# A graph and attention program on one Trainium2 core: a load that is waited for later, a third tile of probabilities, and PSUM banks cleared by two-column products

## What is computed

```python
def _gcn(x, W, b, row, col, ew):            # twice, in the third layer
    x = x @ W
    deg = segment_sum(ew, col) + 1.0
    dinv = rsqrt(deg)
    norm = dinv[row] * ew * dinv[col]
    return segment_sum(norm[:, None] * x[row], col) + (dinv * dinv)[:, None] * x + b
h = relu(x @ Wd + bd) @ Wu + bu + x          # the adapter, ahead of the convolutions
...
attn = softmax(einsum('bhsd,bhtd->bhst', Q, Kt) / sqrt(64))     # fourth layer, 12 heads
attn_out = einsum('bhst,bhtd->bhsd', attn, V)
```

## Time and profile before

| | us |
|---|---|
| timed runs: median (lowest to highest) of 3 | 3585.93 (3583.48 to 3592.32) |
| profiled execution, its own time | 3583.17 |
| its span, first to last instruction | 3581.5 |
| busy in it: TensorE / its weight loads | 2892.7 / 2540.3 |
| busy in it: VectorE / ScalarE / GpSimd | 2028.6 / 1270.8 / 265.5 |
| mean granted TensorE clock (1 is 2.4 GHz, 0.5 is 1.2 GHz) | 0.899 |

### The profile page before, as it was taken

The page is one execution under the profiler, slowest core; times in us unless marked ns, Lnnn a source line. Parts: engine busy times, 40 slices in busy tenths (PEclk is TensorE's granted clock), DMA queues, the critical chain, the costliest instruction groups (busy, mean ns, idle before and its releaser), DMA issues. The chain is left out here.

```text
span 3581.5 us, 42656 instructions
## 1 busy us (share of the span) xinstructions
PE 2892.7 (81%) x15884; PEld 2540.3 (71%) x15885; DVE 2028.6 (57%) x2844; ACT 1270.8 (35%) x1928; POOL 265.5 (7%) x232
## 2 busy tenths in 40 slices
PE   6664887877877859969999986968798699799777
PEld 5553677876877858938888973746666576788776
DVE  6654477877877832253333342363299355688754
ACT  1222275565665521121112110022199101566520
POOL 1332030030030000000000001000000000111100
PEclk9988898988988979979999996978899698899988
DMA  0012111111111172101010022013454120443223
GB/s 29 14 29 50 47 36 59 36 47 59 36 47 59 38 175 52 39 4 51 26 53 26 26 69 53 0 44 120 140 128 88 45 87 0 94 101 76 46 61 91
DMA packets 83081, 204.39 MB, mean 57 GB/s; under 512 B 9866, under 2 KB 39164, under 8 KB 81700
## 3 DMA queue, kind: packets, MB, share of 16 engines
q1 hardware_dynamic: 82950, 202.56, 21.2%
HBM read 153.80 MB, written 44.89 MB: 55 GB/s over the span
## 5 line engine op out<-in xcount | busy, mean ns | idle before, releaser
L831 PE MATMUL ps<-h,e_gat_aggregate 125*125 125x193 f32 x2400 | 408.3, 333 | 90.0 <-DVE e_gat_aggregate L815 73.9
L831 PEld LDWEIGHTS ps<-h,e_gat_aggregate 125*125 125x125 f32 x2400 | 401.8, 192 | 96.8 <-DVE e_gat_aggregate L815 77.8
L103 PE MATMUL ps<-w_pair_experts,hidden_experts 128*125 128x384 f32 x1440 | 257.6, 338 | 5.3 <-DVE x L1237 3.5
L103 PE MATMUL ps<-ln_turned,w_pair_experts 128*128 128x512 f32 (+1 forms) x1296 | 252.0, 356 | 9.4 <-DVE w_pair_experts L1221 9.4
L103 PEld LDWEIGHTS ps<-w_pair_experts,hidden_experts 128*125 128x125 f32 x1440 | 250.7, 185 | 10.5 <-DVE x L1237 6.2
L103 PEld LDWEIGHTS ps<-ln_turned,w_pair_experts 128*128 128x128 f32 x1296 | 212.0, 190 | 50.7 <-DVE w_pair_experts L1221 12.2
L103 PE MATMUL ps<-gat_w_pair_gat_scores,x_turned 128*125 128x384 f32 x1080 | 199.0, 348 | 39.1 <-DVE gat_w_pair_gat_scores L689 38.6
L103 PEld LDWEIGHTS ps<-gat_w_pair_gat_scores,x_turned 128*125 128x125 f32 x1080 | 197.2, 193 | 40.7 <-DVE gat_w_pair_gat_scores L689 39.3
L813 DVE TENSOR_TENSOR e_gat_aggregate<-e_gat_aggregate 125x1250 f32<-125x1250 f32 x120 | 175.2, 1460 | 87.4 <-DMA gat_bias_gat_aggregate<-in_gat_b 48.5
L314 PE MATMUL ps<-dst_hot_build_adjacency,src_hot_build_adjacency 125*125 125x128 bf16 x2380 | 186.1, 235 | 43.4 <-DVE dst_hot_build_adjacency L267 42.4
L777 ACT ACTIVATE e_gat_aggregate<-row_gat_aggregate,from_src 125x1250 f32<-125x1250 f32 x120 | 160.7, 1339 | 166.9 <-PE ps L831 139.3
(11 more groups left out here) (312 smaller groups left out, 4895.4 us busy)
## 6 DMA issues: line engine op xcount, KB each, us to landing
stock<-in_moe_w SPq DMA_DIRECT2D x16, 1152.0 KB, 6.3
row_gat_aggregate<-r_scratch SPq DMA_DIRECT2D x24, 625.0 KB, 6.5
V_home<-q_scratch SPq DMA_DIRECT2D x48, 312.5 KB, 6.5
rows_dense_rows_from<-node_scratch SPq DMA_DIRECT2D x10, 1080.0 KB
stock<-in_gat_w SPq DMA_DIRECT2D x4, 2304.0 KB, 8.5
q_scratch<-V_home SPq DMA_DIRECT2D x6, 1250.0 KB, 4.5
k_scratch<-V_home SPq DMA_DIRECT2D x6, 1250.0 KB, 4.5
V_home<-k_scratch SPq DMA_DIRECT2D x24, 312.5 KB, 6.3
```

The source lines that it names most:

```text
L103: last = pe.matmul(out, left(x), right(y), start=start and n == 0, stop=stop and n == 2)
L831: last = pe.matmul(ps[0:TP, bank(head, d // 2), d % 2 * (C + 1):(d % 2 + 1) * (C + 1)], e[:, n % 3, 0, d * TP:(d + 1) * TP], h[:, t, head, :],
```

## The change

Three edits that don't touch one another:

1. The tile of zeros is 125 x 125 instead of 125 x 512, and each clearing product writes two columns of its bank instead of 512. It still carries `start=True`.
2. The adjacency is no longer in `later`; SP issues its two transfers behind those, with a semaphore of their own (`adj_in`), and doesn't wait for them. VectorE waits for it at the head of `graph_convolutions`.
3. `p`, `p_high`, `p_low` have three buffers (`AHEAD`), TensorE's order is scores(0) to scores(2), and then scores(n+3), weigh(n), the waits hold at n-3, and ScalarE evacuates a head behind the exp of its third following tile (n % 10 == 2) instead of the second.

```diff
-    zeros = ph.sb("zeros", [TP, BANK], BF16)
+    zeros = ph.sb("zeros", [TP, TP], BF16)
...
-                        pe.matmul(ps[0:TP, 3 * odd + b, :], zeros[:, 0:TP], zeros[:], start=True, stop=False,
+                        pe.matmul(ps[0:TP, 3 * odd + b, 0:2], zeros[:], zeros[:, 0:2], start=True, stop=False,
...
             for to, source in later:
                 sp.dma_start(to, source).then_inc(later_in, 16)
+            if behind is not None:
+                to, source, done = behind
+                move_rows(sp, to, source, done)
             if later:
                 sp.wait_ge(later_in, 16 * len(later))
...
         def _(v):
             step = Chain(v, v_step)
+            v.wait_ge(adj_in, 32)
             for t in range(NT):
...
-                (adj[0:EVEN], a_rows[0:EVEN]), (adj[EVEN:TP], a_rows[EVEN:TP])])
+                behind=(adj, a_scratch.rearrange("(t p) d -> p t d", p=TP), adj_in))
...
-    p = ph.sb("p", [TP, 2, NQ])
+    AHEAD = 3
+    p = ph.sb("p", [TP, AHEAD, NQ])
...
-            scores(0)
-            scores(1)
+            for n in range(AHEAD):
+                scores(n)
             for n in range(LAST + 1):
-                if n + 2 <= LAST:
-                    scores(n + 2)
+                if n + AHEAD <= LAST:
+                    scores(n + AHEAD)
                 weigh(n)
...
-                if n >= 2:
-                    a.wait_ge(split, n - 1)
+                if n >= AHEAD:
+                    a.wait_ge(split, n - AHEAD + 1)
...
-                if n % NT == 1 and n >= NT:
+                if n % NT == 2 and n >= NT:
                     evacuate(n // NT - 1)
...
-                if n >= 2:
-                    v.wait_ge(p_used, n - 1)
+                if n >= AHEAD:
+                    v.wait_ge(p_used, n - AHEAD + 1)
```

More of the change, by code:

```diff
@@ L340, in tile_stats, with layernorm_turned @@
     return last
-def layernorm_turned(nc, g, x, turned, gamma=None, beta=None, x_in=None, later=(), stats_there=False):
+def layernorm_turned(nc, g, x, turned, gamma=None, beta=None, x_in=None, later=(), stats_there=False, behind=None):
     ph = Phase(nc, g, "layernorm_turned")
@@ L1853, in attend @@
     ps = g["ps"]
-    p = ph.sb("p", [TP, 2, NQ])
-    p_high = ph.sb("p_high", [TP, 2, NQ], F32R)
-    p_low = ph.sb("p_low", [TP, 2, NQ], F32R)
+    AHEAD = 3
+    p = ph.sb("p", [TP, AHEAD, NQ])
+    p_high = ph.sb("p_high", [TP, AHEAD, NQ], F32R)
+    p_low = ph.sb("p_low", [TP, AHEAD, NQ], F32R)
     k_both = ph.sb("k_high_low", [128, 2, N], F32R)
@@ L1947, in weigh @@
                     for b in range(3):
-                        last = pe.matmul(ps[:, RING + b, 0:PIECE], V[:, t, head, :], tile[:, n % 2, b * PIECE:(b + 1) * PIECE],
+                        last = pe.matmul(ps[:, RING + b, 0:PIECE], V[:, t, head, :], tile[:, n % AHEAD, b * PIECE:(b + 1) * PIECE],
                                          start=(t == 0 and part == 0), stop=(t == NT - 1 and part == 1))
                 last.then_inc(p_used, 1)
-            scores(0)
-            scores(1)
+            for n in range(AHEAD):
+                scores(n)
             for n in range(LAST + 1):
-                if n + 2 <= LAST:
-                    scores(n + 2)
+                if n + AHEAD <= LAST:
+                    scores(n + AHEAD)
                 weigh(n)
@@ L1974, in _ @@
                     bank = (first + at) % RING
-                    last = a.activation(spread(p[:, n % 2, :])[:, at:end, :], ps[0:TP, bank:bank + end - at, 0:PIECE], ACT.Exp, scale=-1.0)
+                    last = a.activation(spread(p[:, n % AHEAD, :])[:, at:end, :], ps[0:TP, bank:bank + end - at, 0:PIECE], ACT.Exp, scale=-1.0)
                 last.then_inc(exp_done, 1)
-                if n % NT == 1 and n >= NT:
+                if n % NT == 2 and n >= NT:
                     evacuate(n // NT - 1)
@@ L1993, in _ @@
                 else:
-                    v.tensor_copy(p_high[:, n % 2, :], p[:, n % 2, :]).then_inc(high_v, 1)
+                    v.tensor_copy(p_high[:, n % AHEAD, :], p[:, n % AHEAD, :]).then_inc(high_v, 1)
                     v.wait_ge(high_v, n - n // 3 + (0 if n % 3 == 2 else 1))
-                v.tensor_tensor(p_low[:, n % 2, :], p[:, n % 2, :], p_high[:, n % 2, :].bitcast(F32), ALU.subtract).then_inc(split, 1)
+                v.tensor_tensor(p_low[:, n % AHEAD, :], p[:, n % AHEAD, :], p_high[:, n % AHEAD, :].bitcast(F32), ALU.subtract).then_inc(split, 1)
     ph.end()
@@ L2205, in build @@
             a_rows = a_scratch.rearrange("(t p) d -> p t d", p=TP)
+            adj_in = gcn.enter_context(nc.semaphore("adjacency_in"))
             layernorm_turned(nc, g, x, g["xT"], later=[
```

12 lines of the change are left out of this document (7 added, 5 removed).

## The result

The changed kernel takes 3557.04 us (median of 4 runs, 3554.03 to 3561.45) where the kernel before took 3585.94 beside it (4 runs, 3583.48 to 3592.32): a ratio of 0.9918, 95% interval 0.99 to 0.9935, so 23 to 36 us faster. The prediction said 3522, with a range of 3504 to 3544. The profiled execution took 3556.27 us.

What follows compares the result with a forecast made beforehand. Stages follow one another behind barriers, so each edit was priced by who waits for whom in its own stage: -13 - 26.4 - 24.5 = -64, giving 3519 us in the profile and 3522 as a median, range 3504 to 3544.

Steps and rivals of the forecast that it cites:

- Edit 2, -26.4: Layer norm ahead of the adapter: the stage ends with ScalarE's work, no longer with the adjacency load, saving 26.4 us.
- the cover of the adapter: Before the convolutions: the adapter's 42 us of matmuls hide the moved wait for the load, with 17.5 us to spare.
- Edit 3, -24.5, bounds -10 and -25: Attend: a third tile gives VectorE's split 2.28 us more lead over GpSimd's adds, saving 24.5 us, between 10 and 25.
- the 20: Attend: of TensorE's 21.6 us of waits for VectorE's split, 20 us go.
- Edit 1, -13: Adjacency: clearing two columns in place of 512 lets later pairs start sooner, saving 13 us.
- Fewer products, lower clock in the adjacency: Rival: less TensorE work drops its clock; at half throughout, +24 for edit 1, total -27, 3559 us; chance 0.10.
- The price of sooner clearing with the clock held: Adjacency: 3.6 us in 14 full-clock windows, 10 in 11 half-clock windows, 0.5 in the last; sum 14, taken as 13.
- GpSimd sets the pair behind the first at full clock: Adjacency: GpSimd's operations hold VectorE's, so sooner clearing saves 0 in about 15 full-clock windows, 0.26 us in 14.
- full clearing: Rival, adjacency: the clearing pays in full, -26 for edit 1, total -77, 3509 us; chance 0.10.
- attend without its lead: Rival, attend: VectorE never regains its lead, so edit 3 gives only -12, total -51, 3535 us; chance 0.13.
- small loads late: Rival, ahead of the adapter: small loads land with the adjacency, edit 2 gives nothing, total -38, 3548 us; chance 0.03.
- GpSimd's addition starved: Rival, attend: GpSimd's add gets in only when VectorE rests, making the kernel slower, +68, 3654 us; chance 0.02.

Runs made afterwards that it cites:

- e2: The kernel before with only the adjacency load taken out of the layer norm's wait: 3558.6 us, ratio 0.9928.
- e5: The changed kernel with three 512-column products of zeros, serving nothing, added behind each adjacency window: 3536.5 us, ratio 0.9864.
- e7: The changed kernel with six 512-column products of zeros, serving nothing, added behind each adjacency window: 3520.3 us, ratio 0.9815.
- e10: The changed kernel with 512-column clearing as before, plus three 512-column products of zeros behind each adjacency window: 3529.6 us, ratio 0.9845.
- e12: The changed kernel with nine 512-column products of zeros, serving nothing, added behind each adjacency window: 3530.2 us, ratio 0.9847.
- e8: The kernel before without GpSimd's two sums per adjacency window, ScalarE copying one of three weight parts instead (result incomplete): 3563.0 us, ratio 0.9934.
- e1: The kernel before with only the banks cleared by two-column products in place of 512: 3614.7 us, ratio 1.0083.
- e11: e7 without GpSimd's two sums per adjacency window, ScalarE copying one of three weight parts instead (result incomplete): 3492.1 us, ratio 0.9745.

## Why the prediction was wrong, point by point

- **What bounds each stage, and the wait that each edit aims at:** right in all three places, in the adjacency only as long as the clock is full.
- **Edit 2, -26.4:** measured -26.7 (and as much alone in e2). The small loads were in before ScalarE ended (SP stood another 10.3 us at the barrier behind them), the cover of the adapter held (0.85 us ahead of L1390, for the barrier), and nothing was given back.
- **Edit 3, -24.5, bounds -10 and -25:** measured -26.3, just beyond the bound. VectorE regained its lead between additions: the waits fell by 20.8 us (21.6 to 0.8), as the 20 had it. By the trace's clock TensorE is at half speed for 15.4 us of the stage before and for 5.0 after, which is worth 5.2 us, and I had 5 for it.
- **Edit 1, -13: this step failed.** It was priced at the granted clock of the kernel before, with one allowance: "since a few more windows may fall to half clock. There the first pair costs nothing more (...), only later pairs do." Not a few windows but 64% of the stage fell, and it cost +26.8 in place of -13. The sum of the profile was -64 and came out at -26.9, 37 us off: 39.8 by this term, less 2.1 that the other two gave beyond theirs and 0.7 in stages that nothing touches. The text had the case as a rival, "Fewer products, lower clock in the adjacency", with +24 for the stage and 3559 for the kernel, at a chance of 0.10. It came out at +26.8 and 3557. Its rate was too low though: it had +24 for a clock at half throughout, and 64% were enough for more. It let the two buffers hide half of what each later pair loses (half of 2.09 - 1.32 is 0.39, and it took 0.3). But the last pair of a window has nothing behind it that could hide anything, and it alone lost 22.3 us in 40 windows, 0.56 each. And a row of 20 took not 2.09 but 2.2 us, in the run of 60 of the timeline above. What the first pairs cost at half clock was forecast rightly as nothing: pauses and first pairs together are 5.1 us shorter than before.
- **How the chance went wrong.** The earlier trace rows gave the sign: a clock of 0.94, that is a stage that fell to half speed from time to time even with the zeros in, and some 26 of TensorE's 220 busy us were to go from it. The section on the clock in the Trainium skill (TensorE: Matmul & The Clock Gate, What's actually happening) was quoted for the rival, and e5 and e7 agree with it: products of zeros that serve nothing lift the clock as well. I gave it 0.10 and did not make it the first question to an edit that takes work off TensorE.
- **The price of sooner clearing with the clock held:** 4.7 us (e10 against e7), where the sum had 3.6 in the windows at full clock, 0.5 in the last, and 10 in the 11 at half clock. The first two terms, 4.1, are about what was measured where every window has a full clock. The 10 could not be measured by themselves, and stay open: e5, at about the old clock, is 4.0 us shorter than the kernel before, which is hardly more than the spread of the lengths. The size of one clearing was off too: mostly 0.42 to 0.47 us from its start to the first count at either clock, not 0.2. It is 0.15 only where TensorE comes to it straight from other products (e12, 282.43 to 282.58).
- **GpSimd sets the pair behind the first at full clock:** right. e8 without the sums gains 21.6 us, within the 15 to 35 expected.
- **The other rivals** (full clearing, attend without its lead, small loads late, GpSimd's addition starved): none came.

The best of the runs that leave nothing out of the computation is e7, the change with six products of zeros behind each window: 3520.3 us, 0.9815 of the kernel before, and about 37 us below the changed kernel by the ratios.

## What to carry to other kernels

Work taken off TensorE can cost more than it saves where TensorE only just keeps its full clock: a granted clock a little under 1.0 in the windows of the stage, 0.94 here, is the warning, and the edit is first priced at the half clock. If the work is in the way, move it into a pause of TensorE, and do not delete it; count what fits in the pause, since three products too many cost 12 us. And where two engines hold each other for one long operation, one more buffer of lead, as long as the operation takes beyond its share, can win nearly all of the stall, as it did here.

## What was not expected of the hardware

- Without its products of zeros TensorE was still busy 257 of 344 us by the profile, with 2.31 us as the longest pause between its products, and yet was granted the full clock for only a third of the time. No longer pause was needed for the fall: in e1, at 0.67, the longest is 1.78 us, and the kernel before has one of 2.08 at 0.94.
- Stretch by stretch the clock sank, from 0.92 to 0.56. It sank in the kernel before as well, from 1.00 to 0.90, and in both the windows shorten from 14 pairs to 2 on the way, so that pauses come more often. That the windows' shape is the reason is not shown; no run here changes their order. Nor do these runs show what it is in TensorE's work that the clock follows.
- A product of two columns is not free: three took 0.28 to 0.48 us busy, and behind a pause the first count started mostly 0.42 to 0.47 us after the first of them. Taking out three times 510 columns saved only 0.26 us per window at full clock (0.69 to 0.43).
- GpSimd's two sums in each window cost 21.6 to 24.0 us of the adjacency (e8 against before, with the clock at 0.97 and 0.94; e11 against e7, both at 1.00), where both of an average window are busy for 1.8 us, 72 in all. No version that moves them and keeps the whole result was tried.
